# An upper end for the limits of the edge groups' node ranges in a four-layer graph network

## The reference

```python
edge_index = jnp.stack([src, dst])
x = _layernorm(x + L0(x))   # attention: softmax over a node's edges, 4 heads, sum of weighted rows
x = _layernorm(x + L1(x))   # sum over edges of x[src], times W_msg, / degree, + x W_self, relu, norm
x = _layernorm(x + L2(x))   # softmax over the source's edges, sum of alpha * x[src], relu
x = _layernorm(x + L3(x))   # per edge x[src] @ W[type] + b[type], max over a node's edges
```

## Time and profile before

| what | us |
|---|---|
| median of 3 runs (5922.94 to 5924.86) | 5922.98 |
| the profiled execution, its own time | 5920.29 |
| its span in the profile | 5917.8 |

### The profile page before, as it was taken

How to read it: one execution, slowest core, us unless ns; L and a number is a source line. 1 busy time by engine, 2 the same in 40 slices (tenths; PEclk the granted TensorE clock), 3 DMA queues, 4 the chain that set the end, 5 groups by cost and what they waited for, 6 DMA issues and landing times. The chain is left out here.

```text
span 5917.8 us, 61603 instructions
## 1 busy us (share of the span) xinstructions
PE 2535.0 (43%) x15195; PEld 2298.0 (39%) x15195; DVE 2020.0 (34%) x5318; ACT 862.9 (15%) x1890; POOL 3293.1 (56%) x3496
## 2 busy tenths in 40 slices
PE   3444444422333333322599953333334433333331
PEld 3444444411333333311599953333332223333331
DVE  3544444422111111145577742222222222222224
ACT  1111111144000000012122210000002411111112
POOL 1777777700777777700011147777773047777776
PEclk6555555555555555555555555555555655655555
DMA  3333333200222212200122322222221135455553
GB/s 81 82 74 73 74 74 74 67 22 22 54 53 52 53 52 53 52 10 10 54 84 84 85 59 53 53 53 53 53 53 45 53 94 131 128 132 133 132 133 103
DMA packets 382812, 414.09 MB, mean 70 GB/s; under 512 B 111946, under 2 KB 281374, under 8 KB 382606
## 3 DMA queue, kind: packets, MB, share of 16 engines
q0 software_dynamic: 108064, 223.66, 16.1%
q1 hardware_dynamic: 268050, 186.77, 11.6%
q10 hardware_dynamic: 6656, 3.21, 0.2%
HBM read 330.84 MB, written 83.80 MB: 70 GB/s over the span
## 5 line engine op out<-in xcount | busy, mean ns | idle before, releaser
L527 POOL DMA_INDIRECT G<-table,IC x3328 | 3145.6, 945 | 1616.5 <-issue 1312.8
L2146 PE MATMUL PS<-SEL,G 128*128 128x96 f32 x1664 | 387.8, 428 | 660.8 <-DVE SEL L2186 660.8
L1317 PE MATMUL PS<-SEL,G 128*128 128x96 f32 x1664 | 384.8, 426 | 661.3 <-DMA G<-table,IC 661.3
L2146 PEld LDWEIGHTS PS<-SEL,G 128*128 128x128 f32 x1664 | 362.7, 330 | 685.9 <-DVE SEL L2186 685.9
L1317 PEld LDWEIGHTS PS<-SEL,G 128*128 128x128 f32 x1664 | 362.7, 330 | 683.4 <-issue 683.4
L989 PE MATMUL PS<-SEL,GW 128*128 128x96 f32 x1664 | 387.8, 428 | 530.1 <-DVEq L1052 530.1
L989 PEld LDWEIGHTS PS<-SEL,GW 128*128 128x128 f32 x1664 | 362.7, 330 | 539.7 <-DVEq L1052 539.7
L2415 DVE TENSOR_TENSOR_SCAN GW<-BIG,GW,PS 128x512 f32<-128x512 bf16 x208 | 266.2, 1280 | 779.3 <-PE PS L2390 758.5
L2390 PE MATMUL PS<-IDENT,G 128*128 128x128 f32 x832 | 204.1, 426 | 679.2 <-DMA G<-table,IC 679.2
L2390 PEld LDWEIGHTS PS<-IDENT,G 128*128 128x128 f32 x832 | 162.6, 223 | 715.9 <-DMA G<-table,IC 531.8
L575 DVE TENSOR_TENSOR BIG<-BIG,PS 128x96 f32 x315 | 79.4, 252 | 902.7 <-PE PS L1317 853.6
(11 more groups left out here) (305 smaller groups left out, 3509.4 us busy)
## 6 DMA issues: line engine op xcount, KB each, us to landing
running_max<-BIG SPq DMA_DIRECT2D x105, 512.0 KB
G<-table,IC POOLq DMA_INDIRECT x3328, 2.5
ROWS<-edge_places SPq DMA_DIRECT2D x209, 192.0 KB, 3.1
G<-source_in_block SPq DMA_DIRECT2D x105, 256.0 KB, 3.3
BIG<-run_mask SPq DMA_DIRECT2D x104, 256.0 KB
table<-BIG SPq DMA_DIRECT2D x49, 256.0 KB
BIG<-xT SPq DMA_DIRECT2D x1, 3125.0 KB, 12.8
BIG<-x SPq DMA_DIRECT2D x24, 128.0 KB, 2.1
```

The costliest lines, as they stand in the source:

```text
L527: pool.indirect_dma_start(out=G[:, b, u, 0:width], out_offset=None, in_=table, in_offset=bass.IndirectOffsetOnAxis(ap=IC[:, b * U + u:b * ...
L1317: last = t.matmul(PS[q][:, 0:W], G[:, b, u, 0:D], SEL[:, q, u, :], start=u == 0, stop=u == U - 1)
L2146: last = t.matmul(PS[q][:, 0:W], G[:, b, u, 0:D], SEL[:, q, u, :], start=u == 0, stop=u == U - 1)
```

## The change

One instruction is added in `edge_lists`. It caps the limits at 5888 (`2 * P * CHUNKS`), the end of the blocks that the chunk of the last turn finishes.

```diff
@@ -313,6 +313,7 @@
                     ch.step(v.tensor_scalar(order_i[:], order_i[:], 2, None, ALU.logical_shift_right))
                     ch.step(v.tensor_copy(order[:], order_i[:]))
                     ch.step(v.tensor_scalar(order[:], order[:], float(2 * P), -4.0 * P, ALU.mult, ALU.add))
+                    ch.step(v.tensor_scalar(order[:], order[:], float(2 * P * CHUNKS), None, ALU.min))
                     dve.wait_ge(rows_in, 64)
                     v.tensor_copy(Fd, Rd)
                     v.tensor_copy(Fp, Rp)
```

## The result

| kernel | median, us | range | runs |
|---|---|---|---|
| before | 5922.96 | 5922.38 to 5924.86 | 4 |
| changed | 5109.75 | 5108.64 to 5111.25 | 4 |

The ratio is 0.8627, with a 95% interval of 0.8612 to 0.8642. The profiled execution of the changed kernel took 5109.49 us, 810.8 us less than that of before; its span is 5107.0 us. Runs further down stand each beside runs of the kernel before on their own chip, since chips differ.

What follows compares the result with a forecast made beforehand. POOL's gathers, 1.25 us each, were taken to pace the edge loops, so other engines' work inside them is free: 5920.3 - 831.5 + 17 + 7.5 + 4 = 5117.3, a median of 5120 us, range 5100 to 5160.

Steps and rivals of the forecast that it cites:

- The flag: In the list test, padding's lowest destination 6176 held flag 4 at 1; the cap at 5888 turns flags 4 and 5 to 0.
- The removed stretches: Between the loops, the node steps of again0, again1 and again2, done with no gather beside them, go away: 831.5 us less.
- What stays of the skipped stages: Between the loops, barriers, flag read and jump of each skipped again stage stay: 5.6 us each, 17 in all.
- The loops' ends: Behind each of three edge loops, skipping the unused form is no longer hidden by gathers: 2.5 us each, 7.5 in all.
- Gathers beside more DVE work: In the edge loops, gathers lengthen in proportion to the chunks' added 295 us of DVE work: 4 us.
- the rule of the rival: In layers 0 and 1, certain DVE node-step operations hold a gather for their full length: 97 us, time 5213; chance 0.07.
- The prediction's other price: In layer 1, by the skill's port lock, a chunk's one fast tensor_scalar costs 7 us, the sum some 3 us more.
- Room on DVE and ACT: In edges0, chunk work fits DVE's 13.3 us of waiting a turn (4.5 taken) and ACT's 8.1 us a group.
- The drain that the prediction allowed for: On ACT in edges0, 1.38 us more at each table set change, 5.3 us a turn with loads; still covered.
- The ring: In the edge loops, a group late by up to 20 us costs nothing on POOL, as its index copy has slack.
- the rival of the dry ring: In the edge loops, index copies over 30 us late make POOL stand 15.9 us a turn: 6217 us; chance 0.02.

Runs made afterwards that it cites:

- runs 1 and 2: Changed kernel with the cap on the limits at 6176, then at 6177, in place of 5888: 5113.81 us, then 5929.91 us.
- run 3: Kernel before, with flag 5 no longer taking in flag 4, so that layer 0 alone runs the first form: 5650.5 us.
- run 8: Changed kernel with the two forms of each edge loop in the other order on each engine: 5113.57 us.
- run 9: Changed kernel with the first form of each edge loop alone, without flag tests, second forms or again stages: 5105.07 us.
- Run 7: Changed kernel without the stages again0, again1 and again2: 5108.6 us.
- run 5: Changed kernel with all four index copies of a turn in edges1 also waiting for the product of the turn's fourth group: 5332.45 us.
- Runs 10 to 12: Half the gathers: kernel before, 4429.1 us; changed kernel on the same chip, 3809.76 us; kernel before again on another chip, 4120.22 us.
- run 4: Changed kernel with ACT doing the index copies of all four groups behind the chunk's steps in each turn of edges1: 5109.86 us.

## Why the prediction was right, step by step

The forecast was 5120, the median is 5109.75: the mechanism held and the sizes of the small terms were 7.8 us too high in sum against the profiled executions (-803.0 forecast, -810.8 found).

*The flag.* Right, and for the reason given: runs 1 and 2 put the turning point at 6176 and 6177.

*The removed stretches.* The 831.5 us are gone from between the loops, and run 3 shows that each layer's part comes by itself: 277 for layer 0, where 276 were expected.

*What stays of the skipped stages.* I had 17, three times 5.6; the gaps are 3.01 + 4.08 + 3.91 = 11.0 us. The sum took the flag read and barrier of a stage that runs and added a whole jump of 2.5 us to them, and that jump was misread. The 2.96 us of the earlier trace rows hold more than a jump. DVE's first row of turn 3 in the changed kernel (a test, no jump), in run 8 (a test, the jump and a second test, as before) and in run 9 (neither):

```profile
260.19 0.48 DVE L630 TENSOR_SCALAR SELT<-ROWS,PART 96x1024 bf16<-96x1024 bf16 x1 [1.74 <-issue]
...
262.96 0.48 DVE L630 TENSOR_SCALAR SELT<-ROWS,PART 96x1024 bf16<-96x1024 bf16 x1 [2.97 <-issue]
...
260.59 0.48 DVE L630 TENSOR_SCALAR SELT<-ROWS,PART 96x1024 bf16<-96x1024 bf16 x1 [0.97 <-issue]
```

The start of a loop alone takes 0.97 us, a test 0.8 us more, and the jump with the second test 1.2 us more. Run 7 has 7.8 us for all three stages in its time and 6.4 in its trace.

*The loops' ends.* I had 7.5 and found 3.3 (+1.5, +2.1, -0.3). The jump shows in layer 0 alone, where run 8 takes it away. There it measures 2.8 us, near the 2.5 that the earlier trace rows had seemed to give, and 1.5 of them reach the loop's end. In layer 1 it is something else: the last product starts late. The end of edges1 in the changed kernel:

```profile
2247.66 0.37 SPq L857 DMA_DIRECT2D target_terms<-BIG  x1
2247.67 0.94 POOL L528 DMA_INDIRECT G<-table,IC  x1 [0.30 <-issue]
...
2253.64 3.70 PE L1318 MATMUL PS<-SEL,G 128*128 128x96 f32 x16 [7.90 <-DMA G<-table,IC]
```

From the last gather's start to the product are 5.97 us. In run 3, where neither a chunk's store nor any other work of a chunk stands there, they are 4.22 (2242.26 to 2246.48). The prediction had said that nothing else is late at the end but layer 2's last store; it had missed this late start, whatever its cause.

*Gathers beside more DVE work.* The net is +4.8 for a forecast of 4, but the rule behind it was wrong. It made the stretch a share of DVE's busy time; yet edges0 got more DVE work and its gathers got 3.1 us shorter, and edges1 took 7.8. In the timeline of edges0 before, some 30 gathers were longer, by 3.0 us together, beside the same DVE operations of a group (L560, L629, L641 of before), and after it 6. The loop's phase against the gathers has moved. So what counts is which operation stands beside a gather, and 4 was right by luck. In edges1 the timeline of the changed kernel has this in each turn:

```profile
2226.16 0.42 DVE L819 TENSOR_TENSOR BIG<-XBUF,BIG 128x256 f32<-128x256 f32 x1
2226.22 1.18 POOL L528 DMA_INDIRECT G<-table,IC  x1 [0.30 <-issue]
2226.72 0.49 DVE L694 BATCH_NORM_STATS2 BN<-BIG 128x6 f32<-128x128 f32 x2
2227.36 0.25 DVE L698 BATCH_NORM_AGGREGATE SM<-BN 128x2 f32<-128x6 f32 x2
```

The gather at that place is 0.2 us longer on average in 23 turns, 4.5 us of the 7.8. That the chunks do it is shown by run 3; which of the three operations does is not. The Trainium skill (SBUF — State Buffer, "Who interferes with whom") says that a DVE instruction with two SBUF inputs contends with GpSimd's reads; L819 is one, all 23 gathers beside it are longer, and the trace agrees as far as that. But a chunk holds seven of that size, and of the 108 gathers that overlap one of them 56 stay under 0.96 us; the others are longer by 0.15 us on average. So the rule of the rival, a gather held for each one's full length (97 us), was some twelve times too high. The prediction's other price, 7 us for the one fast tensor_scalar of a chunk of layer 1, is near the 7.8 in size alone: the 22 gathers that overlap it (L809 here) are longer by 1.7 us together.

*Room on DVE and ACT.* DVE's wait for rows in edges0 is 177.9 / 80 = 2.2 us a group, as forecast, and comes 60 times in 80: before group 1, which the forecast had up to 1 us late, there is none. ACT's wait fell from 8.1 to 4.6 us (364.1 / 80). The drain that the prediction allowed for at a table load isn't seen here either: a copy ends at 305.78 and the root's load starts at 305.80.

*The ring.* The forecast said that lateness up to 20 us costs nothing. No turn of the changed kernel was late enough to matter, as POOL's waits show. Runs 4 and 5 bear it out in edges1: 11 us cost nothing and leave 13.8, and 34 us cost 10.6, so the cover is some 24 us. Behind it the loss is real, 10.6 us a turn in run 5, which is near the 11.6 us of standing a turn at which the rival of the dry ring would have decided: 69 such turns would have eaten 730 of the 811 us.

*Where it would have been wrong.* Runs 10 to 12 show how far the cover reaches. With half the gathers, and on a chip that was slow from the start, the same node steps give back 199 us inside the loops.

## What to carry to other kernels

Work of other engines is free inside a loop bound by one engine's transfers as long as the loop's own waits are longer than the work, which the waits of each engine show before anything is changed. A run-time test that picks the fast form should be tried with the padding rows too: here a few groups of padding and one constant decided nearly 14% of the time, and nothing but idle POOL stretches told of it. Price a lateness from the wait that each consumer really has, not from the length of the chain that was moved: run 4 was mis-sized by three times that way. And ask which transfer reads the result: a releaser's name beside the usual 0.3 us is no wait.

## What I had not expected of the hardware

A store of 1.5 KB in small pieces beside a gather goes with rows that are late. Two groups' products in a turn of edges1 in the changed kernel's timeline, with that store between them:

```profile
2200.15 3.70 PE L1318 MATMUL PS<-SEL,G 128*128 128x96 f32 x16 [4.36 <-DMA G<-table,IC]
...
2207.40 0.37 SPq L857 DMA_DIRECT2D target_terms<-BIG  x1
...
2213.15 3.70 PE L1318 MATMUL PS<-SEL,G 128*128 128x96 f32 x16 [7.64 <-DMA G<-table,IC]
```

Products follow one another by 10.0 us, and this one comes after 13.0; the next one, at 2220.19, comes after 7.0 and has made it up. The same stands in the turn before (2159.83, 2172.74, 2179.93), and in run 3's edges1, without chunks and stores, all products but the last are 10.0 us apart (2195.12 to 2235.01). The store itself takes 5.4 us to land. I ran no kernel without the store alone, so that it is the cause is argued from its place. Inside the loop it costs nothing, at the end 1.75 us.

Testing a flag, jumping over an unused form and testing once more costs DVE 2.0 us over a loop without tests (2.97 against 0.97), the jump over the same form behind edges0 held it for 2.8 us, and a whole skipped stage with both barriers leaves only 3 to 4 us between two stages' work. One chip took 6789 us for a kernel that took 5923 to 5930 on the others.
